# Strips written out in place of a loop, and gates spread by pairs of experts into a ring of six pairs

## The chip, the cores and the metric

The kernel runs on one core of one Trainium2 chip. A core has five engines that run side by side, each with its own list of instructions: TensorE (PE in the profile; its weight loads are PEld), VectorE (DVE), ScalarE (ACT), GpSimd (POOL) and SyncE (SP), which here issues every DMA. They wait for each other by semaphores. The metric is the device time of the whole program in microseconds (us), the median of several runs.

## The reference

The input x has the shape (4, 64, 128, 128). Two residual blocks are applied to it, window attention and a mixture of experts:

```python
x = x + attention(_ln_c(x), ...)      # 8x8 windows, 4 heads of 16 channels, relative position bias
t = _to_tokens(x)                     # 4 x 16384 tokens of 64 channels
t = t + ffn(_ln_t(t), ...)

# ffn
router_probs = softmax(x @ router_w + router_b)      # 8 experts
top_p, top_i = top_k(router_probs, 2)
top_p = top_p / sum(top_p)
expert_out = einsum('bnd,edc->bnec', x, expert_w) + expert_b
out = einsum('bnk,bnkc->bnc', top_p, take_along_axis(expert_out, top_i[..., None], axis=2))
```

All arithmetic is in float32. `_ln_c` and `_ln_t` take the mean away over the channels and divide by the standard deviation.

## The kernel before

**Strips.** The work is cut into 32 strips. A strip is eight rows (one row of windows) of two images; the two images' channels take the 128 partitions (image `a` has partitions 64a to 64a+63), and the 8 x 128 = 1024 pixels lie along the row (`LT`). A strip passes through seven stages, and in each step of the program every engine works on up to seven strips, `s[0]` to `s[6]`, where `s[k]` is the strip that was loaded k steps ago. `s[2]` and `s[3]` are in attention, `s[4]` gets its residual, its router and its gates, `s[5]` goes through the experts and is finished, `s[6]` is stored. There are 38 steps. Each engine's order within a step is written out by hand in its last function (L376, L625, L814, L918, L1108).

**The loop.** `steps` (L264) writes out steps 0 to 9, runs steps 10 to 29 as a hardware loop of five rounds of U = 4 steps, and writes out steps 30 to 37. In the loop the values that semaphores are waited for depend on the round, so registers are computed, and x is loaded and stored at addresses from registers. There are four jumps back.

**Gates.** For each token the two chosen experts have a gate and the other six have zero. The chain that makes them, per strip: TensorE transposes the router's output (`transpose_logits`, L588), VectorE finds the top two (L1060 to L1106), GpSimd places the gates (`place_gates`, L898 to L909), TensorE transposes them (`transpose_gates`, L595 and L597), ScalarE moves them to SBUF (`move_gates`, L812), SyncE writes them to DRAM (`write_gates`, L329) and reads them back, each expert's row of 1024 gates copied to all 64 partitions of its image (`spread_gates`, L347). The tile `gz` has eight buffers of one expert each. Per expert there are two DMAs, one for each image, of 64 rows of 4 KB. Then the token tile `tt` is multiplied into the buffer in place (`gated`): experts 1, 4 and 7 on GpSimd (L915), 0, 2, 3, 5 and 6 on VectorE (L1026). TensorE multiplies each expert's buffer by its weights and adds all up in PSUM (`experts`, L620), and `finish` (L1034) adds the residual.

**Order around it.** On VectorE the end of a step is `normalise` 3, `gated` 0, `finish` of the strip before, `gated` 2; the next step begins with `row_max` 2 (L1005), `shift` 2 (L1012), `gated` 3, `gated` 5, `variance` (L986). On TensorE a step begins with `experts` 0, transposes and channel sums, `scores_left` 3 (L516, which needs `shift` 2), values, the router, `scores_right` 3, transposes, `transpose_logits` (L588, which needs a PSUM bank that `variance` frees). GpSimd does the residual (L889), `gated` 1, `gated` 4, later `place_gates` and `gated` 7. On SyncE the spreads of experts 0 to 5 end the step, and 6 and 7 begin the next one, followed by the store, the load of x, `swap_tokens` and `load_gate_rows`.

## Time and profile before

| | us |
|---|---|
| median of 3 runs | 1319.18 |
| lowest and highest | 1318.9, 1325.99 |
| the profiled execution | 1319.76 |
| its span, first to last instruction | 1317.8 |
| TensorE, VectorE busy | 1108.7 (84%), 920.3 (70%) |
| ScalarE, GpSimd busy | 707.6 (54%), 439.8 (33%) |
| SyncE's DMA queue | 217.32 MB, 66.3% of 16 DMA engines |
| mean granted TensorE clock | 0.934 |

No engine is busy all the time; the strips' chains through several engines and the DMA queue set the pace. A step is best read from one mark per step, for instance the start of ScalarE's move of the projection (L779), and within a step from T, the start of the first DMA that spreads the strip's gates. The granted clock is 1.0 at 2.4 GHz and 0.5 at 1.2 GHz.

### The profile page before, as it was taken

How to read it: one execution, taken by the hardware profiler on the slowest of the kernel's cores; microseconds unless marked ns; L12 is line 12 of the kernel's file. 1: busy time of each engine (PE TensorE's matmuls, PEld its weight loads, DVE VectorE, ACT ScalarE, POOL GpSimd, SP SyncE). 2: the span in 40 equal slices, each digit the busy share in tenths (PEclk: the TensorE clock that was granted, in tenths of full speed). 3: DMA queues.
4: the chain of work that ended last, by engine and by line, in shares of the span. 5: the costliest groups of instructions: out<-in, count | busy, mean ns of one | idle time of the engine just before them, and what ended most of it. 6: DMA issues, size and time to landing. Idle time of an engine off the chain costs nothing.

```text
span 1317.8 us, 41226 instructions
## 1 busy us (share of the span) xinstructions
PE 1108.7 (84%) x16678; PEld 578.2 (44%) x16678; DVE 920.3 (70%) x1398; ACT 707.6 (54%) x1153; POOL 439.8 (33%) x359
## 2 busy tenths in 40 slices
PE   4688998888899979987998879899799889988754
PEld 2344444444444434443544435444344444444311
DVE  3247787778777767885778757777677877776642
ACT  1366565555565646654665546665466566555410
POOL 1003234433443233343234424432343344233342
PEclk9999899999999989998999989999899999998877
DMA  3216676777766658877576777776588777755676
GB/s 127 65 42 155 147 183 174 179 199 189 197 159 173 174 143 199 198 195 188 123 184 171 180 183 190 169 177 173 136 199 200 194 188 162 172 146 143 153 174 169
DMA packets 91494, 219.85 MB, mean 167 GB/s; under 512 B 17728, under 2 KB 30656, under 8 KB 91200
## 3 DMA queue, kind: packets, MB, share of 16 engines
q1 hardware_dynamic: 91328, 217.32, 66.3%
q8 instruction: 143, 2.34, 0.8%
q14 instruction: 23, 0.19, 0.1%
HBM read 177.15 MB, written 23.33 MB: 152 GB/s over the span
## 4 chain that ended last, share of the span: by engine, by line
PE 44%; DMA 26%; issue 11%; SPq 9%; DVE 6%; ACT 2%; POOL 1%; POOLq 0%; DVEq 0%; ACTq 0%
DMA gz<-gates_dram 22%; PE bank L620 14%; SPq L347 8%; PE bank L501 6%; PE bank L462 5%; PE bank L534 5%; PE bank L551 3%; PE bank L558 3%; DMA gates_dram<-gsb 3%; PE bank L489 3%; PE bank L516 2%; DVE mx L1005 2%; DVE probs L1012 2%; PE bank L588 2%; DVE gz L1026 1%
## 5 line engine op out<-in xcount | busy, mean ns | idle before, releaser
L1026 DVE TENSOR_TENSOR gz<-gz,tt 128x1024 f32<-128x1024 f32 x160 | 301.6, 1889 | 127.3 <-DMA gz<-gates_dram 127.2
L620 PE MATMUL bank<-gz,wex 64*64 64x512 f32 x2048 | 276.8, 648 | 47.7 <-issue 33.2
L915 POOL TENSOR_TENSOR gz<-gz,tt 128x1024 f32<-128x1024 f32 x96 | 250.4, 2619 | 23.9 <-DMA gz<-gates_dram 23.9
L889 POOL TENSOR_TENSOR tt<-prj,xs 128x512 f32<-128x512 f32 x64 | 106.3, 1681 | 437.1 <-ACT prj L779 437.1
L762 ACT ACTIVATE pt<-bank 128x512 f32<-128x512 f32 x256 | 150.5, 588 | 106.4 <-PE bank L534 106.4
L1005 DVE TENSOR_REDUCE mx<-bank 128x16 f32<-128x1024 f32 x128 | 155.6, 1216 | 58.4 <-PE bank L501 58.4
L1012 DVE TENSOR_TENSOR probs<-bank,mx 128x1024 f32<-128x1024 f32 x128 | 156.7, 1224 | 43.3 <-PE bank L534 34.3
L501 PE MATMUL bank<-km,qs 32*64 32x128 f32 x4096 | 177.7, 289 | 3.4 <-issue 0.5
L534 PE MATMUL bank<-cst,probs 128*128 128x128 f32 x1024 | 173.3, 293 | 5.1 <-ACT pt L762 5.1
L501 PEld LDWEIGHTS bank<-km,qs 32*64 32x64 f32 x4096 | 113.4, 136 | 111.4 <-issue 100.1
L534 PEld LDWEIGHTS bank<-cst,probs 128*128 128x128 f32 x1024 | 110.7, 144 | 114.3 <-issue 48.0
L898 POOL TENSOR_TENSOR ga<-oh,g 128x128 f32<-128x128 f32 x32 | 13.9, 434 | 400.9 <-DVE g L1106 400.9
L620 PEld LDWEIGHTS bank<-gz,wex 64*64 64x64 f32 x2048 | 71.8, 142 | 171.3 <-issue 169.7
L516 PE MATMUL bank<-bias_hl,tile_id 128*128 128x512 f32 x256 | 93.3, 447 | 60.0 <-DVE probs L1012 54.6
L755 ACT ACTIVATE probs<-probs 128x1024 f32<-128x1024 f32 x128 | 134.8, 1053 | 6.9 <-DVE probs L1012 6.2
L769 ACT ACTIVATE rden<-bank 128x256 f32<-128x256 f32 x128 | 49.1, 383 | 109.4 <-PE bank L558 109.4
L551 PE MATMUL bank<-pt,vbd 128*32 128x64 f32 x4096 | 94.5, 229 | 1.5 <-ACT pt L762 1.5
L1020 DVE TENSOR_TENSOR onrm<-bank,rden 128x256 f32<-128x256 f32 x128 | 54.0, 422 | 52.0 <-ACT rden L774 51.7
L462 PE MATMUL bank<-xr,wcen 64*64 64x512 f32 x512 | 74.2, 655 | 10.1 <-DVE var L986 5.8
L558 PE MATMUL bank<-pt,cst 128*32 128x256 f32 x1024 | 80.2, 385 | 0.0
L740 ACT ACTIVATE km<-bank,hmask 128x1024 f32<-128x1024 f32 x64 | 67.8, 1110 | 23.0 <-PE bank L462 23.0
L551 PEld LDWEIGHTS bank<-pt,vbd 128*32 128x32 f32 x4096 | 67.2, 113 | 28.4 <-issue 23.5
(95 smaller groups left out, 1259.8 us busy)
## 6 DMA issues: line engine op xcount, KB each, us to landing
gz<-gates_dram SPq DMA_DIRECT2D x512, 256.0 KB, 7.9
xs<-in_x SPq DMA_DIRECT2D x32, 512.0 KB, 10.6
rstd<-std_dram SPq DMA_DIRECT2D x64, 256.0 KB, 4.0
tx<-tt SPq DMA_DIRECT2D x128, 128.0 KB, 9.2
out<-ob SPq DMA_DIRECT2D x128, 128.0 KB, 9.1
gates_dram<-gsb SPq DMA_DIRECT2D x32, 192.0 KB, 2.1
grow<-gates_dram SPq DMA_DIRECT2D x192, 32.0 KB
gz<-in_rel SPq DMA_DIRECT2D x1, 2048.0 KB, 8.8
```

The lines of the kernel that those rows point to most:

```text
L462: last = mm(bank[64 * x:64 * x + 64, PRE + a, :], wcen[64 * a:64 * a + 64, at + 64 * a:at + 64 * a + 64], xr[s.buf(2)][64 * a:64 * a + 64, ...
L501: last = mm(bank[N * j:N * j + N, S_BANK + hp, 256 * x + 128 * ii:256 * x + 128 * ii + 128], qs[32 * r:32 * r + 32, a, w, :], km[32 * r:32 ...
L534: last = nc.tensor.transpose(bank[:, PT_BANK, 128 * r:128 * r + 128], probs[g % 2][:, r % 2, r // 2, u % 2, :], cv("ident"))
L551: mm(bank[32 * r:32 * r + 32, OD_BANK, at:at + N], vbd[:, CW * (r // 2) + w, 2 * a + r % 2, :, :].rearrange("p m d -> p (m d)"), pt[g % 2] ...
L558: last = mm(bank[32 * r:32 * r + 32, OD_BANK, 256:512], cv("pair"), pt[g % 2][:, :, r, :, :], start=True, stop=True, skip_group_check=True)
L620: last = mm(bank[64 * x:64 * x + 64, Y_BANK + a, :], wex[64 * a:64 * a + 64, e, :], gz[64 * a:64 * a + 64, e, x * CH:(x + 1) * CH], start= ...
L755: af(v, v, ACT.Exp).then_inc(exp_done, 1)
L762: af(pt[g % 2][:, u % 2, :, :, :].rearrange("p r j q -> p (r j q)"), bank[:, PT_BANK, :], ACT.Copy).then_inc(pt_ready, 1)
L915: tt_(gz[:, e, :], gz[:, e, :], tt[s.buf(4)][:, :], op=ALU.mult).then_inc(z_pool, 1)
L1005: red(mx[g % 2][:, :], two_banks(S_BANK).rearrange("p (c k) -> p c k", k=N), axis=AX_X, op=ALU.max).then_inc(max_done, 1)
L1012: tt_(probs[g % 2][:, :, :, :, :].rearrange("p h x i (m k) -> p (h x i m) k", k=N), two_banks(S_BANK).rearrange("p (c k) -> p c k", k=N), ...
L1026: tt_(gz[:, e, :], gz[:, e, :], tt[s.buf(4)][:, :], op=ALU.mult).then_inc(z_dve, 1)
```

## The change

Three things are changed, and the order of work on each engine stays.

1. All 38 steps are written out. The loop, its registers, its jumps and the semaphores `waited` and `sp_waited` are gone, and all waits are for constants.
2. `gz` has six buffers of two experts each (48 KB of a partition in place of 32 KB). Pair q of strip c uses buffer (4c + q) mod 6. Per pair there are two DMAs, one for each image, of 64 rows of 8 KB, so eight DMAs for a strip in place of sixteen. `gated` waits for the pair that holds its expert. A pair's load waits until the pair that had the buffer six pairs earlier has been used up.
3. To make room, `lnv`, `L2` and `cand` are dropped: `msq`, `Ls` and `eq` are written again in their place.

```diff
-        gz = sb("gz", [P, E, LT])
+        gz = sb("gz", [P, GZ_RING, 2, LT])
...
+            def pair(self, e):
+
+                return divmod(4 * self.c + e // 2, GZ_RING)
...
-            for i in range(lo):
-                run(Step(i, 0, False))
-            with nc.Fori(0, n, engines=(run.engine,)) as r:
-                for v in range(U):
-                    run(Step(lo + v, r, True))
-            for i in range(lo + n * U, last + 1):
-                run(Step(i, 0, False))
...
+        def stepped(f):
+            for c in range(STRIPS + LAST_STAGE):
+                f(Step(c))
+            return f
...
-            def spread_gates(s, e):
-
-                if e == 0:
+            def spread_gates(s, q):
+
+                if q == 0:
                     sp.wait_ge(gates_written, s.count(16, 16))
-                    sp.sem_inc(sp_waited, 1)
-                wait(sp, e_done, s.count(E, e + 1, lag=1))
+
+                wait(sp, e_done, 2 * (s.count(4, q) - GZ_RING + 1))
+                k = s.count(4, q) % GZ_RING
                 for a in range(2):
-                    sp.dma_start(gz[64 * a:64 * a + 64, e, :],
-                                 gates_dram[s.buf(4), 0, E * a + e, :].partition_broadcast(64)
-                                 ).then_inc(gz_loaded[e], 16)
+                    sp.dma_start(gz[64 * a:64 * a + 64, k, :, :].rearrange("p e t -> p (e t)"),
+                                 gates_dram[s.buf(4), 0, E * a + 2 * q:E * a + 2 * q + 2, :].rearrange(
+                                     "e t -> (e t)").partition_broadcast(64)).then_inc(gz_loaded[k], 16)
...
                 if s[5].on:
-                    spread_gates(s[5], 6)
-                    spread_gates(s[5], 7)
+                    spread_gates(s[5], 3)
...
-                pool.wait_ge(gz_loaded[e], s.count(32, 32))
-                tt_(gz[:, e, :], gz[:, e, :], tt[s.buf(4)][:, :],
+                use, k = s.pair(e)
+                pool.wait_ge(gz_loaded[k], 32 * use + 32)
+                tt_(gz[:, k, e % 2, :], gz[:, k, e % 2, :], tt[s.buf(4)][:, :],
                     op=ALU.mult).then_inc(z_pool, 1)
...
-                dve.wait_ge(gz_loaded[e], s.count(32, 32))
-                tt_(gz[:, e, :], gz[:, e, :], tt[s.buf(4)][:, :],
+                use, k = s.pair(e)
+                dve.wait_ge(gz_loaded[k], 32 * use + 32)
+                tt_(gz[:, k, e % 2, :], gz[:, k, e % 2, :], tt[s.buf(4)][:, :],
                     op=ALU.mult).then_inc(z_dve, 1)
```

**The queue of SyncE.** First one written-out step of before, from the write of the gates to DRAM, then the same place now:

```order
L329 DMA gates_dram<-gsb 128x3x128
L347 DMA gz<-gates_dram 64x1024 x16
L367 DMA out<-ob 64x512 x4
L308 DMA xs<-in_x 128x1024
L356 DMA tx<-tt 64x512 x4
```

```order
L304 DMA gates_dram<-gsb 128x3x128
L323 DMA gz<-gates_dram 64x2048 x8
L343 DMA out<-ob 64x512 x4
L284 DMA xs<-in_x 128x1024
L332 DMA tx<-tt 64x512 x4
```

Nothing has moved; sixteen DMAs of 64 x 1024 elements have become eight of 64 x 2048.

**VectorE around the step's boundary**, a written-out place, with the semaphores that each row waits for (`gz_loaded2` belongs to expert 2 before, and to the buffer that pair 2 of one strip or another uses now). Before:

```order
L1026 TENSOR_TENSOR gz<-gz,tt3 128x1024 [waits gz_loaded0]
L1034 TENSOR_TENSOR ob0<-bank,tx 128x1024 [waits stored0,tx_loaded0,y_full]
L1026 TENSOR_TENSOR gz<-gz,tt3 128x1024 [waits gz_loaded2]
L1005 TENSOR_REDUCE mx0<-bank 128x16 [waits s_full]
L1012 TENSOR_TENSOR probs0<-bank,mx0 128x1024 [waits t_full,max_done]
L1026 TENSOR_TENSOR gz<-gz,tt3 128x1024 [waits gz_loaded3]
L1026 TENSOR_TENSOR gz<-gz,tt3 128x1024 [waits gz_loaded5]
L986 TENSOR_TENSOR var<-bank,msq 128x256 [waits std_written,msq_ready]
```

Now (the strip shown uses the buffers 0, 1 and 2 for its pairs 0, 1 and 2):

```order
L997 TENSOR_TENSOR gz<-gz,tt3 128x1024 [waits gz_loaded0]
L1005 TENSOR_TENSOR ob0<-bank,tx 128x1024 [waits stored0,tx_loaded0,y_full]
L997 TENSOR_TENSOR gz<-gz,tt3 128x1024 [waits gz_loaded1]
L975 TENSOR_REDUCE mx0<-bank 128x16 [waits s_full]
L982 TENSOR_TENSOR probs0<-bank,mx0 128x1024 [waits t_full,max_done]
L997 TENSOR_TENSOR gz<-gz,tt3 128x1024 [waits gz_loaded1]
L997 TENSOR_TENSOR gz<-gz,tt3 128x1024 [waits gz_loaded2]
L956 TENSOR_TENSOR var<-bank,msq 128x256 [waits std_written,msq_ready]
```

The order is the same. The first `gated` now waits for experts 0 and 1 together, the second for 2 and 3, the fourth for 4 and 5.

**TensorE at the loop's end**, before:

```order
L534 MATMUL bank<-cst,probs 128x128 x4
L524 REGISTER_ALU
L501 MATMUL bank<-km,qs 64x128 x8
L271 REGISTER_ALU
L271 COMPARE_AND_BRANCH
L620 MATMUL bank<-gz,wex 64x512 x4
```

Now there is no register operation and no branch between the steps; the matmuls stand in the same order.

## Rows read from the trace of the kernel before

**Rows 1.** The page: shares of engines and of the chain that ended last.

```profile
PE 1108.7 (84%) x16678; PEld 578.2 (44%) x16678; DVE 920.3 (70%) x1398; ACT 707.6 (54%) x1153; POOL 439.8 (33%) x359
PE 44%; DMA 26%; issue 11%; SPq 9%; DVE 6%; ACT 2%; POOL 1%; POOLq 0%; DVEq 0%; ACTq 0%
DMA gz<-gates_dram 22%; PE bank L620 14%; SPq L347 8%; PE bank L501 6%; PE bank L462 5%; PE bank L534 5%; PE bank L551 3%; PE bank L558 3%; DMA gates_dram<-gsb 3%; PE bank L489 3%; PE bank L516 2%; DVE mx L1005 2%; DVE probs L1012 2%; PE bank L588 2%; DVE gz L1026 1%
```

**Rows 2.** Timeline of ScalarE, L779, once per step: start, duration, what, [idle before].

```profile
196.94 1.11 ACT L779 ACTIVATE prj<-bank,sml 128x1024 f32<-128x1024 f32 x1 [0.75 <-PE bank L569]
...
346.88 1.11 ACT L779 ACTIVATE prj<-bank,sml 128x1024 f32<-128x1024 f32 x1 [0.75 <-PE bank L569]
...
612.28 1.11 ACT L779 ACTIVATE prj<-bank,sml 128x1024 f32<-128x1024 f32 x1 [0.75 <-PE bank L569]
...
654.62 1.11 ACT L779 ACTIVATE prj<-bank,sml 128x1024 f32<-128x1024 f32 x1 [0.76 <-PE bank L569]
...
1073.08 1.11 ACT L779 ACTIVATE prj<-bank,sml 128x1024 f32<-128x1024 f32 x1 [0.75 <-PE bank L569]
...
1223.00 1.11 ACT L779 ACTIVATE prj<-bank,sml 128x1024 f32<-128x1024 f32 x1 [0.75 <-PE bank L569]
```

**Rows 3.** A jump back: TensorE's timeline, and its line in the waits.

```profile
621.74 1.98 PE L620 MATMUL bank<-gz,wex 64*64 64x512 f32 x8 [8.34 <-issue]
...
PE bank L620 <- issue: 33.2, 5, 8.3
```

**Rows 4.** Timeline of SyncE's queue in one step, from T = 338.47, and its wait there.

```profile
335.96 0.41 SPq L329 DMA_DIRECT2D gates_dram<-gsb  x1
338.47 10.99 SPq L347 DMA_DIRECT2D gz<-gates_dram  x16
349.72 2.53 SPq L367 DMA_DIRECT2D out<-ob  x4
352.56 0.37 SPq L308 DMA_DIRECT2D xs<-in_x  x1
...
375.78 0.45 SPq L347 DMA_DIRECT2D gz<-gates_dram  x1
...
SPq L347 <- PE bank L620: 10.1, 22, 1.4
```

**Rows 5.** DMA in windows 340.3:340.7, then 342.9:343.3: issue to landing of one DMA.

```profile
gz<-gates_dram SPq DMA_DIRECT2D x1, 256.0 KB, 5.5
...
gz<-gates_dram SPq DMA_DIRECT2D x1, 256.0 KB, 8.6
```

**Rows 6.** VectorE's timeline in the same step.

```profile
343.51 1.23 DVE L1026 TENSOR_TENSOR gz<-gz,tt 128x1024 f32<-128x1024 f32 x1
344.86 1.23 DVE L1034 TENSOR_TENSOR ob<-bank,tx 128x1024 f32<-128x1024 f32 x1
349.17 1.34 DVE L1026 TENSOR_TENSOR gz<-gz,tt 128x1024 f32<-128x1024 f32 x1 [3.08 <-DMA gz<-gates_dram]
350.43 1.21 DVE L1005 TENSOR_REDUCE mx<-bank 128x16 f32<-128x1024 f32 x1
351.76 1.22 DVE L1012 TENSOR_TENSOR probs<-bank,mx 128x1024 f32<-128x1024 f32 x1
352.90 2.13 DVE L1026 TENSOR_TENSOR gz<-gz,tt 128x1024 f32<-128x1024 f32 x1
355.80 2.55 DVE L1026 TENSOR_TENSOR gz<-gz,tt 128x1024 f32<-128x1024 f32 x1 [0.76 <-DMA gz<-gates_dram]
358.27 0.41 DVE L986 TENSOR_TENSOR var<-bank,msq 128x256 f32<-128x256 f32 x1
```

**Rows 7.** GpSimd's timeline in the same step: experts 1 and 4.

```profile
351.60 2.35 POOL L915 TENSOR_TENSOR gz<-gz,tt 128x1024 f32<-128x1024 f32 x1
...
353.91 3.35 POOL L915 TENSOR_TENSOR gz<-gz,tt 128x1024 f32<-128x1024 f32 x1
```

**Rows 8.** TensorE's timeline there, and ScalarE's row of the gates.

```profile
353.04 0.73 PE L516 MATMUL bank<-bias_hl,tile_id 128*128 128x512 f32 x2 [1.85 <-DVE probs L1012]
...
356.12 0.66 PE L534 MATMUL bank<-cst,probs 128*128 128x128 f32 x4
358.83 1.08 PE L588 MATMUL bank<-cst,lg 128*128 128x128 f32 x4 [2.06 <-DVE var L986]
...
373.04 0.49 ACT L812 ACTIVATE gsb<-bank 128x384 f32<-128x384 f32 x1
```

**Rows 9.** A shorter step: half clock ahead of L588 (last row: windows, clock 0.50).

```profile
508.43 0.92 PE L516 MATMUL bank<-bias_hl,tile_id 128*128 128x512 f32 x2 [1.85 <-DVE probs L1012]
...
513.05 0.66 PE L534 MATMUL bank<-cst,probs 128*128 128x128 f32 x4
514.21 0.63 PE L588 MATMUL bank<-cst,lg 128*128 128x128 f32 x4 [0.51 <-DVE var L986]
...
526.98 0.49 ACT L812 ACTIVATE gsb<-bank 128x384 f32<-128x384 f32 x1
...
508.80:512.21 3.41, 3.41 (x42) 1.36 (x40) 2.97 (x2) 0.07 (x1) 3.41 (x2) 0.50 1.04 231
```

**Rows 10.** DMA packets in windows 303:318, 320:322 and 9:13.

```profile
DMA packets 1076, 3.55 MB, mean 237 GB/s; under 512 B 213, under 2 KB 213, under 8 KB 1075
...
DMA packets 340, 0.81 MB, mean 405 GB/s; under 512 B 57, under 2 KB 57, under 8 KB 339
...
DMA packets 122, 1.72 MB, mean 430 GB/s; under 512 B 8, under 2 KB 8, under 8 KB 20
```

More of the change, by code:

```diff
@@ L47, in build_program @@
     PAIRS = B // 2
+    GZ_RING = 6
     LAST_STAGE = 6
@@ L210, in build_program @@
         gates_written, grow_loaded = sem("gates_written"), sem("grow_loaded")
-        gz_loaded = [sem(f"gz_loaded{e}") for e in range(E)]
+        gz_loaded = [sem(f"gz_loaded{k}") for k in range(GZ_RING)]
         z_dve, z_pool, e_done, y_full, y_ready = (sem("z_dve"), sem("z_pool"), sem("e_done"), sem("y_full"),
@@ L227, in build_program, with __init__ @@
         }
-        class Step:
-            def __init__(self, c, n, inner):
-                self.c, self.n, self.inner = c, n, inner
-            def strips(self):
-                return [Strip(self.c - k, self.n, self.inner) for k in range(LAST_STAGE + 1)]
         class Strip:
-            def __init__(self, c, n, inner):
-                self.c, self.n, self.inner = c, n, inner
-                self.on = inner or 0 <= c < STRIPS
+            def __init__(self, c):
+                self.c = c
+                self.on = 0 <= c < STRIPS
             def buf(self, k):
@@ L248, in count, with __init__, strips @@
             def count(self, per, k, lag=0):
-                v = per * (self.c - lag) + k
-                return v + per * U * self.n if self.inner else v
+                return per * (self.c - lag) + k
             def rounds(self, k, of):
-                v = of * (self.c // k)
-                return v + of * (U // k) * self.n if self.inner else v
-        def wait(eng, s, value):
-            if isinstance(value, int) and value <= 0:
-                return
-            eng.wait_ge(s, value)
-        def steps(run):
-            last = STRIPS - 1 + LAST_STAGE
-            lo = LAST_STAGE + 4
-            n = (STRIPS - lo) // U
-            for i in range(lo):
-                run(Step(i, 0, False))
-            with nc.Fori(0, n, engines=(run.engine,)) as r:
-                for v in range(U):
-                    run(Step(lo + v, r, True))
-            for i in range(lo + n * U, last + 1):
-                run(Step(i, 0, False))
-        def stepped(engine_type):
-            def mark(f):
-                class Run:
-                    engine = engine_type
-                    def __call__(self, st):
-                        f(st)
-                steps(Run())
-            return mark
+                return of * (self.c // k)
+            def pair(self, e):
+                return divmod(4 * self.c + e // 2, GZ_RING)
+        class Step:
+            def __init__(self, c):
+                self.c = c
+            def strips(self):
+                return [Strip(self.c - k) for k in range(LAST_STAGE + 1)]
+        def wait(eng, s, value):
+            if value > 0:
+                eng.wait_ge(s, value)
+        def stepped(f):
+            for c in range(STRIPS + LAST_STAGE):
+                f(Step(c))
+            return f
         block = ctx.enter_context(nc.Block())
-        ET = mybir.EngineType
         @block.sync
@@ L374, in late_loads @@
                     sp.dma_start(dst, src).then_inc(late_loaded, 16)
-            @stepped(ET.SP)
+            @stepped
             def _(st):
@@ L439, in free @@
                     _, back, s, per = rounds[at]
-                    if st.inner or 0 <= c - back < STRIPS:
-                        wait(pe, s, Strip(c - back, st.n, st.inner).count(per, per))
+                    if 0 <= c - back < STRIPS:
+                        wait(pe, s, Strip(c - back).count(per, per))
                         return
@@ L1089, in top_two @@
             def top_two(s):
-                top_step(s, 10, nc.vector.scalar_tensor_tensor(out=L2[:, :, :], in0=oh1[:, :, :], scalar=-BIG,
+                top_step(s, 10, nc.vector.scalar_tensor_tensor(out=Ls[:, :, :], in0=oh1[:, :, :], scalar=-BIG,
                                                                in1=L[:, :, :], op0=ALU.mult, op1=ALU.add))
-                candidates(s, 10, L2, m2)
+                candidates(s, 10, Ls, m2)
             def pick_two(s):
```

41 lines of the change are left out of this document (14 added, 27 removed).

## The prediction

> **What bounds the kernel now.** I read the page first. TensorE is busy 84% and VectorE 70%, so neither fills the span, and the chain that ended last holds 22% of DMA of the spread gates and 8% of their issue beside TensorE's lines [rows 1]. So each strip's gates go round a circle, and the circle's length is a step. The next view is one mark per step. Eight written-out steps on either side of the loop (196.94 to 346.88 and 1073.08 to 1223.00) take 299.86 us, 37.48 each. The 19 steps between, which hold the loop's jumps, take 726.20 us, where 19 at 37.48 would be 712.1. One step with a jump takes 654.62 - 612.28 = 42.3 us [rows 2], and TensorE idles 8.34 us in it without a releaser; 33.2 us of such idle time stand in the waits, five times, four of them jumps [rows 3].
>
> Then the circle itself, in one step, with T = 338.47, the first spread DMA [rows 4]. Expert 1 lands at 340.24 + 5.5 = T+7.3, expert 3 at 342.80 + 8.6 = T+12.9 (issued in the 10.99 us burst, one DMA each 0.64 us) [rows 4, 5]. VectorE multiplies expert 0 at T+5.0, finishes the older strip by T+7.6, waits 3.08 us for expert 2 until T+10.7, does the maximum and the shift until T+14.5, expert 3, waits 0.76 us for expert 5 until T+17.3, and starts the variance at T+19.8 [rows 6]. TensorE waits twice: 1.85 us for the shift, starting at T+14.6, and 2.06 us for the variance, until L588 at T+20.4. From L588 the top two, the gates and their transposes lead to L812 at 373.04, which is 14.2 us later [rows 8], and 2.74 us after that the next strip's spread starts, at 375.78 [rows 4]. 20.4 + 14.2 + 2.7 = 37.3. Both of VectorE's waits end with a landing, so landings set the circle.
>
> **The clock in it.** In a step in the loop L588 comes only 0.51 us after its predecessor, because TensorE ran at clock 0.50, 1.2 GHz, from 508.80 to 512.21, after its 1.85 us wait; from there to L812 it is 526.98 - 514.21 = 12.8 us, not 14.2 [rows 9]. So a stretch at half clock costs some 1.4 us behind L588 and nothing ahead of it, where the wait for the variance hides it. The written-out steps have mostly the first kind.
>
> **Part 1, the loop written out.** The matmuls and their order are the same, and the written-out steps of before already show what steps without a jump cost. Replacing the 19 looped steps by steps of 37.48 us removes 726.2 - 712.1 = 14.1 us. That is less than four times 42.3 - 37.5 = 4.8, since some looped steps after a jump are short ones of 36.1, with the half clock hidden. Registers and added semaphore steps cost nothing that I can see: the looped steps without a jump are no longer than written-out ones. The trace shows the stall at the jump itself as 8.34 us of idle TensorE [rows 3]. The Trainium skill, in "Runtime: NRT & Kernel Launch", section "Instruction fetch mechanics", says that a taken branch breaks the sequential prefetch; the trace agrees with it, but adds that half of the stall is caught up.
>
> **Part 2, pairs: what falls away.** Eight DMAs fewer are issued per strip, at 0.64 us each 5.1 us of SyncE's queue. I cost this at nothing. The DMA engines are the cover: over 303 to 318 they move 237 GB/s [rows 10], so the strip's 4.19 MB take 17.7 us, longer than the issue's 11. Behind the burst on SyncE stands the store, which must wait for `finish` (which part 3 ends at T+10.6) and starts at T+11.2 today, so the queue gains no time for it; x and the tokens queue behind the same bytes. The wait for a free buffer is gone too: it was 10.1 us over the whole run, in 22 pieces [rows 4], and the same backlog hid it. The aliases of `msq`, `Ls` and `eq` join operations that already follow each other on one engine, and cost nothing.
>
> **Part 3, pairs: what comes later.** Bytes and order are kept, so pair q lands when its second expert landed: pair 0 at T+7.3 (7.3 to 8.4 over the strips), pair 1 at T+12.9, pair 2 at T+17.3, as expert 5 does. The steps on VectorE are then:
> - `gated` 0 starts at T+8.0 in place of 5.0, `finish` ends at T+10.6. `experts` 0 on TensorE, which follows the free PSUM bank, slips by 0.9 us into the wait for the shift, where it is hidden; if that wait were gone it would cost its 0.9.
> - `gated` 2 starts at T+12.9 in place of 10.7. It now lies beside `gated` 1 on GpSimd, so I take 2.13 us for it, as `gated` 3 had beside GpSimd, not 1.34 [rows 6, 7]. Then maximum and shift, 2.4 us: T+17.4 in place of 14.5. TensorE's first wait grows from 1.85 to about 3.5 us.
> - `gated` 4 on GpSimd starts with pair 2, at T+17.3 in place of 15.4, and takes 3.35 us beside VectorE: T+20.7. `gated` 3 runs to T+19.5, and `gated` 5 ends 1.1 us after GpSimd's operation, as it does now (358.35 against 357.26): T+21.7 [rows 6, 7]. The variance starts there, and L588 0.56 us later: T+22.3 in place of 20.4.
> So the wait of 0.76 is gone, but the operations are squeezed behind a later pair 1 and a later `gated` 4: +1.9 us on this leg.
>
> **What the clock gives back.** TensorE's work between its two waits is 3.7 us at full clock (353.04 to 356.78) [rows 8] and 5.3 us with the half clock in it (508.43 to 513.71) [rows 9]. With one long wait ahead of it the half clock moves mostly ahead of L588. Then L588 is at the later of T+22.3 and 17.5 + 5.3 = T+22.8, and the circle is 22.8 + 12.8 + 2.7 = 38.3. With the stretch hidden partly in the long wait it is 22.3 + 12.8 + 2.7 = 37.8; with it behind L588 still, 39.2. I take 38.05, between the first two, since the wait becomes longer than either was. Over about 28 steps (the first and last few have fewer stages) this is 28 x (38.05 - 37.48) = +16 us.
>
> **Sum.** 1319.76 - 14.1 + 16 = 1321.7 for the profiled execution, which stands 0.6 above the median of the three; I say **1321**, no change. The unknown that counts most is the rate at which rows of 8 KB move. From above, 430 GB/s: one broadcast DMA of 16 KB rows to 128 partitions had it [rows 10]. From below, half of that, 215. I stay at 237, by the nearest row: the same 64-partition broadcasts. Each per cent of it moves pair 2 by 0.13 us and the run by 3.7 us.
>
> On that rate two rules can be weighed. The broadcast to all 128 partitions moved 430 GB/s, and the two broadcasts to 64 each only 237, at full DMA share in both [rows 10]. The Trainium skill, "DMA: Bandwidth & Descriptors", section "The descriptor swizzle", has the partitions 0 to 63 behind one half of the ports and 64 to 127 behind the other; by this a 64-partition DMA has half of the ports whatever its row's length, and the sum stays.
>
> **The rivals.**
> - *Rows of 8 KB move faster* (faster). For it: packets of 4 KB move at 237 GB/s, of 16 KB at 430 [rows 10], and eight completions per strip fall away. Against: those 16 KB went to 128 partitions, and 405 GB/s were reached at 320 to 322 by stores and x with rows of 2 and 4 KB. With 10% more, pair 1 lands at T+11.9 and pair 2 at T+16.0; L588 follows at 20.9 to 21.8, a circle of 36.5 to 37.3, and the run at 1319.8 - 14.1 - 28 x 0.6 = 1289. By the Trainium skill, "DMA: Bandwidth & Descriptors", section "Rules for kernel authors", bigger DMAs have more bandwidth; that would be this rival.
> - *The later landing is absorbed* (faster). If the half clock falls wholly into the long wait and VectorE and GpSimd hinder each other less, the circle stays at 37.5, and the loop's share is left: 1319.8 - 14.1 = 1306.
> - *The two halves' packets overlap less* (slower). 237 is over 215, so today the packets for the lower and the upper 64 partitions overlap somewhat. With four packets of 8 KB per DMA and engine they may do so for a smaller share. At 222 GB/s pair 2 lands 0.9 us later, all of it is on the leg, and the half clock can fall behind L588: a circle of 39.1 and 1319.8 - 14.1 + 28 x 1.6 = 1350. It decides from a rate under 233, where the steps add over 0.5%.
> - *The written-out code stalls*: each engine streams more code. The written-out steps show no idle time of this kind; a stall in each of 20 steps of 1 us would give 1341.
>
> **How the numbers follow.** Forecast 0.45, with a range of its own of 1310 to 1334; of it 0.30 within 0.5%, 0.12 slower, 0.03 faster. Faster rows 0.22; absorbed 0.10; less overlap 0.19, code 0.04. A measurement of this kernel can tell about 0.5% from no change, 6.6 us. Faster 0.35, same 0.30, slower 0.35. The range 1288 to 1348 takes in the likelier parts of both sides and leaves a tenth out at either end.
>
> **What would show it.** After the change no idle time of 8 us at a step's start. VectorE's idle time before `gated` 0 and `gated` 2 by landings at T+8 and T+12.9, none before `gated` 5; one wait of TensorE of over 3 us at L516 and under 1 us at L588; `gated` 4 at pair 2's landing; the rate in the burst at 237. A rate above 250 or below 230 makes the forecast wrong, and so would steps of another length at the same landings.

## The result, and the profile after

The changed kernel takes **1367.16 us** (median, 1365.24 to 1367.37) where the kernel before takes 1321.96 in the same comparison: a ratio of 1.034, with an interval of 1.030 to 1.037. It is slower, and outside the predicted range of 1288 to 1348. The profiled execution has a span of 1363.3 us, 45.5 more than before. Executions of one kernel fall into a faster and a slower state, and ratios go by the faster ones; the profiled executions of two runs below, e3 (1273.2 us) and e10 (1354.9 us), and one more of e3's four runs, were slower ones.

The page of the changed kernel, in the order of [rows 1]: busy time of engines, then the chain that ended last. After it, the kind of transfer that is spread per pair, with the KB and the median us from issue to landing.

```profile
PE 1121.5 (82%) x16678; PEld 591.5 (43%) x16678; DVE 947.2 (69%) x1398; ACT 709.3 (52%) x1153; POOL 408.6 (30%) x359
...
PE 43%; DMA 33%; DVE 8%; issue 7%; SPq 5%; ACT 2%; POOL 1%; POOLq 0%; DVEq 0%
...
gz<-gates_dram SPq DMA_DIRECT2D x256, 512.0 KB, 12.0
```

The DMA's share of the chain has risen from 26% to 33%. TensorE is busy 13 us more than before, VectorE 27 us more and GpSimd 31 us less, at the same work. The marks of the steps (ScalarE's move of the projection, as [rows 2]):

```profile
203.61 1.11 ACT L748 ACTIVATE prj<-bank,sml 128x1024 f32<-128x1024 f32 x1 [0.75 <-PE bank L539]
242.38 1.11 ACT L748 ACTIVATE prj<-bank,sml 128x1024 f32<-128x1024 f32 x1 [0.75 <-PE bank L539]
282.36 1.12 ACT L748 ACTIVATE prj<-bank,sml 128x1024 f32<-128x1024 f32 x1 [0.75 <-PE bank L539]
321.11 1.11 ACT L748 ACTIVATE prj<-bank,sml 128x1024 f32<-128x1024 f32 x1 [0.75 <-PE bank L539]
...
1265.49 1.12 ACT L748 ACTIVATE prj<-bank,sml 128x1024 f32<-128x1024 f32 x1 [0.75 <-PE bank L539]
```

Most steps alternate between 38.8 us and 39.5 to 40.0. Over the same 27 steps, (1265.49 - 203.61)/27 = 39.33, where before had (1223.00 - 196.94)/27 = 38.00 [rows 2]. So 45.5 splits into 35.8 in the 27 steps (1.33 each), 6.7 ahead of the first mark and 3.0 behind the last.

Now one step, with T = 352.15, the start of the first spread DMA. SyncE's queue, as [rows 4]:

```profile
350.07 0.39 SPq L304 DMA_DIRECT2D gates_dram<-gsb  x1
352.15 4.92 SPq L323 DMA_DIRECT2D gz<-gates_dram  x8
361.87 2.85 SPq L343 DMA_DIRECT2D out<-ob  x4
```

VectorE, as [rows 6], and GpSimd, as [rows 7]:

```profile
359.48 1.23 DVE L997 TENSOR_TENSOR gz<-gz,tt 128x1024 f32<-128x1024 f32 x1 [1.83 <-DMA gz<-gates_dram]
360.62 1.22 DVE L1005 TENSOR_TENSOR ob<-bank,tx 128x1024 f32<-128x1024 f32 x1
365.28 2.80 DVE L997 TENSOR_TENSOR gz<-gz,tt 128x1024 f32<-128x1024 f32 x1 [3.44 <-DMA gz<-gates_dram]
368.01 1.21 DVE L975 TENSOR_REDUCE mx<-bank 128x16 f32<-128x1024 f32 x1
369.25 1.22 DVE L982 TENSOR_TENSOR probs<-bank,mx 128x1024 f32<-128x1024 f32 x1
370.39 4.37 DVE L997 TENSOR_TENSOR gz<-gz,tt 128x1024 f32<-128x1024 f32 x2
374.69 0.41 DVE L956 TENSOR_TENSOR var<-bank,msq 128x256 f32<-128x256 f32 x1
```

```profile
364.64 2.37 POOL L885 TENSOR_TENSOR gz<-gz,tt 128x1024 f32<-128x1024 f32 x1
370.19 2.36 POOL L885 TENSOR_TENSOR gz<-gz,tt 128x1024 f32<-128x1024 f32 x1 [3.19 <-DMA gz<-gates_dram]
```

`gated` 0 starts at T+7.3 and `finish` ends at T+9.7. `gated` 2 starts at T+13.1 and ends at 368.08, T+15.9; that is 1.07 us after the end of GpSimd's `gated` 1 (367.01), which ran beside it. The shift ends at T+18.3. TensorE then, as [rows 8], in this step and the next (whose T is 390.98). L487 is `scores_left` 3 and L558 is `transpose_logits`, which were L516 and L588 before. ScalarE's move of the gates to `gsb` and the windows of both stretches at half clock follow (the last three columns are clock, DMA share and GB/s):

```profile
370.53 1.22 PE L487 MATMUL bank<-bias_hl,tile_id 128*128 128x512 f32 x2 [5.24 <-DVE probs L982]
...
375.73 0.60 PE L558 MATMUL bank<-cst,lg 128*128 128x128 f32 x4
...
409.36 1.22 PE L487 MATMUL bank<-bias_hl,tile_id 128*128 128x512 f32 x2 [5.23 <-DVE probs L982]
...
415.50 0.60 PE L558 MATMUL bank<-cst,lg 128*128 128x128 f32 x4
```

```profile
388.38 0.49 ACT L781 ACTIVATE gsb<-bank 128x384 f32<-128x384 f32 x1
...
428.15 0.49 ACT L781 ACTIVATE gsb<-bank 128x384 f32<-128x384 f32 x1
```

```profile
367.36:374.20 6.84, 3.67 (x42) 1.86 (x42) 6.80 (x5) 0.00 (x0) 2.36 (x1) 0.50 0.98 235
...
408.30:415.14 6.84, 5.78 (x59) 2.81 (x60) 5.61 (x5) 1.14 (x2) 2.36 (x1) 0.50 1.00 288
```

TensorE waits 5.24 us for the shift in place of 1.85 [rows 8], and the wait for the variance is gone. It then runs at 1.2 GHz until 374.20 in the first step, and until 415.14 in the second. L558 therefore starts at T+23.6 in the one and T+24.5 in the other; 12.65 us lie from there to `gsb` in both, and 2.6 from `gsb` to the next T: 38.8 and, within 0.1, 39.8 us, the two lengths of the steps. So the circle that the prediction read is longer at two places, the end of `gated` 2 and the half clock.

The waits of the whole run (total us, times, longest), the second of them 54.6 in the kernel before; and the DMA packets of one burst, as [rows 10]:

```profile
DVE gz L997 <- DMA gz<-gates_dram: 198.6, 67, 13.4
...
PE bank L487 <- DVE probs L982: 135.9, 34, 5.2
POOL gz L885 <- DMA gz<-gates_dram: 124.7, 34, 8.6
```

```profile
DMA packets 494, 3.27 MB, mean 218 GB/s; under 512 B 96, under 2 KB 96, under 8 KB 96
```

218 GB/s where there were 237 [rows 10]. Over strips 3 to 28 the pairs land at T+7.7, 13.2, 18.1 and 22.4 on average; before, experts 1, 3, 5 and 7 landed at 7.9, 12.8, 17.3 and 20.9.

### The profile page after: what moved, and what is told of

It reads as the page before. It is cut to its first block, busy times and chain, and to the rows that moved or that the text cites. A ratio compares the mean times of both kernels' runs of the same rounds, so it can differ in the third digit from the quotient of the medians.

```text
span 1363.3 us, 38803 instructions
## 1 busy us (share of the span) xinstructions
PE 1121.5 (82%) x16678; PEld 591.5 (43%) x16678; DVE 947.2 (69%) x1398; ACT 709.3 (52%) x1153; POOL 408.6 (30%) x359
## 4 chain that ended last, share of the span: by engine, by line
PE 43%; DMA 33%; DVE 8%; issue 7%; SPq 5%; ACT 2%; POOL 1%; POOLq 0%; DVEq 0%
DMA gz<-gates_dram 27%; PE bank L589 10%; PE bank L472 7%; PE bank L505 6%; DMA gates_dram<-gsb 5%; SPq L323 4%; PE bank L433 4%; PE bank L487 4%; PE bank L522 4%; PE bank L548 3%; DVE probs L982 3%; DVE mx L975 3%; PE bank L529 2%; ACT gsb L781 1%; PE bank L558 1%
## 5 line engine op out<-in xcount | busy, mean ns | idle before, releaser
L997 DVE TENSOR_TENSOR gz<-gz,tt 128x1024 f32<-128x1024 f32 x160 | 325.1, 2047 | 198.8 <-DMA gz<-gates_dram 198.6
L589 PE MATMUL bank<-gz,wex 64*64 64x512 f32 x2048 | 262.8, 615 | 39.8 <-DVE ob L1005 33.4
L885 POOL TENSOR_TENSOR gz<-gz,tt 128x1024 f32<-128x1024 f32 x96 | 243.4, 2535 | 124.7 <-DMA gz<-gates_dram 124.7
L487 PE MATMUL bank<-bias_hl,tile_id 128*128 128x512 f32 x256 | 102.2, 484 | 143.0 <-DVE probs L982 135.9
L858 POOL TENSOR_TENSOR tt<-prj,xs 128x512 f32<-128x512 f32 x64 | 82.1, 1305 | 434.4 <-ACT prj L748 434.4
L472 PE MATMUL bank<-km,qs 32*64 32x128 f32 x4096 | 192.3, 308 | 2.9
L472 PEld LDWEIGHTS bank<-km,qs 32*64 32x64 f32 x4096 | 123.2, 146 | 129.1 <-issue 117.8
L759 ACT ACTIVATE lg<-bank 128x512 f32<-128x512 f32 x32 | 19.1, 597 | 238.2 <-PE bank L550 238.2
L589 PEld LDWEIGHTS bank<-gz,wex 64*64 64x64 f32 x2048 | 70.9, 135 | 159.7 <-issue 144.1
L487 PEld LDWEIGHTS bank<-bias_hl,tile_id 128*128 128x128 f32 x256 | 45.2, 210 | 163.5 <-DVE probs L982 154.1
L522 PE MATMUL bank<-pt,vbd 128*32 128x64 f32 x4096 | 97.5, 234 | 1.5 <-ACT pt L731 1.5
## 6 DMA issues: line engine op xcount, KB each, us to landing
xs<-in_x SPq DMA_DIRECT2D x32, 512.0 KB, 12.8
```

Of the source, the lines that this page charges most:

```text
L472: last = mm(bank[N * j:N * j + N, S_BANK + hp, 256 * x + 128 * ii:256 * x + 128 * ii + 128], qs[32 * r:32 * r + 32, a, w, :], km[32 * r:32 ...
L487: mm(bank[:, S_BANK + hp, :], tile_id[:, :], bias_hl[:, 2 * hp:2 * hp + 2, :].rearrange("p h k -> p (h k)").unsqueeze(1).broadcast_to([P, ...
L522: mm(bank[32 * r:32 * r + 32, OD_BANK, at:at + N], vbd[:, CW * (r // 2) + w, 2 * a + r % 2, :, :].rearrange("p m d -> p (m d)"), pt[g % 2] ...
L589: last = mm(bank[64 * x:64 * x + 64, Y_BANK + a, :], wex[64 * a:64 * a + 64, e, :], gz[64 * a:64 * a + 64, s.pair(e)[1], e % 2, x * CH:(x ...
L885: tt_(gz[:, k, e % 2, :], gz[:, k, e % 2, :], tt[s.buf(4)][:, :], op=ALU.mult).then_inc(z_pool, 1)
L997: tt_(gz[:, k, e % 2, :], gz[:, k, e % 2, :], tt[s.buf(4)][:, :], op=ALU.mult).then_inc(z_dve, 1)
```

## The experiments

Ratios are to the kernel before, run on the same chip; steps are means over the same 27 steps of the profiled execution.

| run | what it is | us | ratio, interval | steps |
|---|---|---|---|---|
| before | | 1319 | 1 | 38.0 |
| e11_ring8 | written out, eight single buffers | 1289.99 | 0.976, 0.971 to 0.981 | 37.2 |
| e1_single | the same, ring of twelve experts | 1296.13 | 0.980, 0.975 to 0.985 | 37.4 |
| e2_pairwait | e1, waits per pair | 1344.57 | 1.018, 1.012 to 1.023 | 38.9 |
| e10_quarter | after, 256 KB DMAs of 32 partitions | 1340.35 | 1.013, 1.009 to 1.018 | 39.0 |
| after | | 1367.16 | 1.034, 1.030 to 1.037 | 39.3 |

**e1_single: single experts, written out.** Does the loop or the spread make the difference?

```diff
-                for a in range(2):
-                    sp.dma_start(gz[64 * a:64 * a + 64, k, :, :].rearrange("p e t -> p (e t)"), ...)
+                for e in (2 * q, 2 * q + 1):
+                    wait(sp, e_done, 8 * s.c + e - 2 * GZ_RING + 1)
+                    for a in range(2):
+                        sp.dma_start(gz[64 * a:64 * a + 64, k, e % 2, :],
+                                     gates_dram[s.buf(4), 0, E * a + e, :].partition_broadcast(64)
+                                     ).then_inc(gz_loaded[2 * k + e % 2], 16)
```

> The written-out program with the ring kept (twelve single buffers), but each expert's gates are again two DMAs of 64 rows of 4 KB with a semaphore of their own. Both theories (the pairs' coarser waits cost the time; the pairs' lower DMA rate costs it) expect the same: steps of 37.5 us, a rate of 237 GB/s in the burst and 1306 us, within 1298 to 1320: the loop's share alone, 0.99 of before. A third theory, that the written-out code itself costs time, expects over 1340.

Measured: 1296.13 us, 0.980, just under what was expected (1298 to 1320), since the loop's share is larger. Landings and rate are those of before (expert 5 at T+17.1, 236 GB/s in the burst). So all of the loss is in the pairs, and they cost 71 us, not 16.

**e2_pairwait: DMAs per expert, waits per pair.** Of the pairs only the coarser wait is left.

```diff
-                                     ).then_inc(gz_loaded[2 * k + e % 2], 16)
+                                     ).then_inc(gz_loaded[k], 16)
...
-                dve.wait_ge(gz_loaded[2 * k + e % 2], 32 * use + 32)
+                dve.wait_ge(gz_loaded[k], 64 * use + 64)
```

> DMAs of 64 rows of 4 KB, one per expert and image as before, but the engines wait for both experts of a pair. Rate theory: the rate is 237 GB/s again, the pairs land at about T+7.6, 12.9 and 17.3, and only the grouping is paid, a circle of 38.2 to 38.6 us and 1325 to 1337 us in all. Grouping theory (the waits are the whole cost): 1355 to 1370 us, as the changed kernel.

Measured: 1344.57 us, 1.018, between what the two theories gave. The rate is that of before, and pairs land at T+8.1, 12.5 and 16.9 in the strip of T = 342.54. VectorE, GpSimd and TensorE in it:

```profile
355.05 3.44 DVE L998 TENSOR_TENSOR gz<-gz,tt 128x1024 f32<-128x1024 f32 x1 [2.04 <-DMA gz<-gates_dram]
358.41 1.21 DVE L976 TENSOR_REDUCE mx<-bank 128x16 f32<-128x1024 f32 x1
```

```profile
355.04 2.37 POOL L886 TENSOR_TENSOR gz<-gz,tt 128x1024 f32<-128x1024 f32 x1
```

```profile
360.93 1.06 PE L488 MATMUL bank<-bias_hl,tile_id 128*128 128x512 f32 x2 [4.52 <-DVE probs L983]
...
366.04 0.60 PE L559 MATMUL bank<-cst,lg 128*128 128x128 f32 x4
```

`gated` 2 starts at T+12.5 together with GpSimd's `gated` 1 and lasts 3.44 us, until T+15.9, as late as in the changed kernel although pair 1 lands 0.6 us sooner. The coarser wait alone costs 48 us.

`gated` 2 doesn't end so late in every step. GpSimd can start `gated` 1 at T+12.5, when the residual is done. In the strip of T = 693.94 pair 1 lands at T+12.42, just ahead of that, and VectorE gets in first (VectorE, GpSimd, TensorE):

```profile
706.39 1.23 DVE L998 TENSOR_TENSOR gz<-gz,tt 128x1024 f32<-128x1024 f32 x1 [2.03 <-DMA gz<-gates_dram]
```

```profile
706.44 3.38 POOL L886 TENSOR_TENSOR gz<-gz,tt 128x1024 f32<-128x1024 f32 x1
```

```profile
710.06 0.73 PE L488 MATMUL bank<-bias_hl,tile_id 128*128 128x512 f32 x2 [2.29 <-DVE probs L983]
```

Now VectorE's product takes 1.23 us and GpSimd's 3.38, and TensorE goes on at T+16.1 in place of 18.4. Of strips 3 to 28 this happens in five here, with steps of 36.3 to 37.7 us, in four of e10 below, and in none of the changed kernel, where pair 1 lands at T+12.7 or later.

**e4_rows4k: the changed kernel's eight DMAs with rows of 4 KB.** The buffer is laid out so that a pair's two experts aren't adjacent; DMAs, bytes and waits stay.

```diff
-        gz = sb("gz", [P, GZ_RING, 2, LT])
+        gz = sb("gz", [P, 2, GZ_RING, LT])
...
-                    sp.dma_start(gz[64 * a:64 * a + 64, k, :, :].rearrange("p e t -> p (e t)"), ...)
+                    sp.dma_start(gz[64 * a:64 * a + 64, :, k, :],
+                                 gates_dram[s.buf(4), 0, E * a + 2 * q:E * a + 2 * q + 2, :].partition_broadcast(64)
+                                 ).then_inc(gz_loaded[k], 16)
```

> The pairs' eight DMAs of 512 KB and the pairs' waits are kept, but a pair's two experts lie apart in SBUF, so each row is two packets of 4 KB. If the packet's length sets the rate: 237 GB/s again and 1325 to 1337 us. If the bytes that one DMA writes to one half of the partitions set it: 218 GB/s and 1360 to 1370 us, as the changed kernel.

Measured: 1363.57 us, 1.034 (1.031 to 1.037); pairs land at T+8.0, 13.5, 18.4 and 22.7. The packets' length is not the cause; the DMA of 512 KB is what e2 and e4 still differ in.

**e10_quarter: pieces of 256 KB with rows of 8 KB.** The other half of the same question.

```diff
-                for a in range(2):
-                    sp.dma_start(gz[64 * a:64 * a + 64, k, :, :].rearrange("p e t -> p (e t)"), ...)
+                for h in range(2):
+                    for a in range(2):
+                        sp.dma_start(gz[64 * a + 32 * h:64 * a + 32 * h + 32, k, :, :].rearrange("p e t -> p (e t)"),
+                                     ...partition_broadcast(32)).then_inc(gz_loaded[k], 16)
```

> The changed kernel, with each pair loaded by four DMAs of 32 partitions (256 KB each, rows of 8 KB as in the changed kernel), the two images in turn, in place of two DMAs of 64 partitions (512 KB). Theory: the size of the piece that goes to one half of the partitions before the other half's turn sets the rate. Then pieces of 256 KB bring back what e2_pairwait had: landings at T+7.9, 12.5, 17.0, 20.8, 237 GB/s in the burst, about 1345 us. Rival: rows of two experts or the coarser semaphore are slower whatever the piece is, or the 32 partitions are reached by fewer ports: landings as in the changed kernel or later (pair 2 at T+18 or more), 1362 us or more.

Measured: 1340.35 us, 1.013. The landings are e2's, T+7.6, 12.5, 17.0 and 20.9 (e2 has 7.9, 12.5, 17.0 and 20.8), and the burst has 237 GB/s again:

```profile
DMA packets 648, 3.56 MB, mean 237 GB/s; under 512 B 215, under 2 KB 215, under 8 KB 215
```

Rate and landings go with the size of the DMA, and so of the piece that each half of the partitions gets in turn, not with the rows; size and turns weren't varied apart. It costs 23 to 27 us (after against e2 and e10), each difference uncertain by some 8 us; between the profiled executions of e2 and the changed kernel it is 18. In e2's five steps in which VectorE got in first, 11 us are saved against 39.3, which is all that its 27 steps are shorter by (10.6). So read from these steps, the later landing costs time by losing this race, and not by its 0.7 us: where GpSimd is first at T+12.5, `gated` 2 ends at T+15.9, early landing or late.

**e11_ring8: the steps written out, without the larger ring.** As e1, with `GZ_RING = 4`, which is eight buffers. The reuse of `msq`, `Ls` and `eq` (part 3 of the change) stays.

> The steps written out and nothing else: eight buffers of one expert, DMAs and semaphores for each expert as in the kernel before (e1_single had twelve buffers). Theory: what e1_single gained (ratio 0.980, -23 us by its medians) is the loop's share alone, since the waits for a free buffer were 10 us in 22 pieces behind a backlog: 1293 to 1300 us, waits of SyncE for TensorE again at the spread. Rival: part of it is the ring's, and the loop's share is the 14 us of the prediction: 1305 to 1310 us.

Measured: 1289.99 us, 0.976, a little under the 1293 expected. The four more buffers of e1 bring nothing, and the loop's share is 22 us between the profiled executions (spans of 1317.8 and 1295.4) and 30 between the medians.

**e3_onesource: one DMA to all 128 partitions.** Both images get the first image's gates; the second image's own are left out.

```diff
-                for a in range(2):
-                    sp.dma_start(gz[64 * a:64 * a + 64, k, :, :].rearrange("p e t -> p (e t)"), ...)
+                sp.dma_start(gz[:, k, :, :].rearrange("p e t -> p (e t)"), ...
+                                 "e t -> (e t)").partition_broadcast(128)).then_inc(gz_loaded[k], 16)
```

> Each pair is one DMA with rows of 8 KB to all 128 partitions, from image 0's gates; the second image gets the first one's gates, which is left wrong, the bytes written are the same. Theory that a DMA to 64 partitions is held back by its destination half: the rate rises to 350 to 430 GB/s, pair 1 lands by T+8, pair 2 by T+11, VectorE waits for no landing after the first, and the time falls under 1290 us (steps of 35 to 36.5 us). Theory that many engines reading one source row hold it back: the rate stays near 220 GB/s and the time at 1355 to 1370 us.

Measured: 0.956 (0.948 to 0.964); the median of all four runs is 1271.35 us. Same bytes written, same rows of 8 KB, and the burst moves

```profile
DMA packets 735, 4.27 MB, mean 388 GB/s; under 512 B 95, under 2 KB 95, under 8 KB 255
```

with the last pair at T+14.8 in place of 22.4. So the 218 GB/s are a matter of the 64 partitions of one DMA, as far as this run tells: it also has half as many DMAs, of twice the size, and half as many source rows. By the Trainium skill, "DMA: Bandwidth & Descriptors", section "The descriptor swizzle", each half of the partitions has its own half of the ports, and this run agrees.

**e5_skew4k: the burst begun unevenly.** e1 with one DMA from DRAM to DRAM of 8 rows of 16 KB ahead of each burst.

```diff
+                    wait(sp, padded, s.count(16, 0))
+                    sp.dma_start(pad_dram, x_rows[0:8, 0:4096]).then_inc(padded, 16)
```

> The single-expert version (1296 us), with one DMA more ahead of each strip's burst, from DRAM to DRAM, of 8 rows of 16 KB (data that nobody uses), so that half of the DMA engines start the burst late by what one 64-partition DMA gives each engine. If the engines that share a destination port hinder each other because they are in step, the burst then moves at 350 to 430 GB/s, pair-wise landings come by T+6, T+8 and T+11, and the time falls by 5 to 30 us. If the engines fall back into step or do not pair like this, the rate stays at 237 GB/s and the time rises by the added issue, 0.5 us per step, 1296 to 1312.

Measured: 1301.34 us, 0.979 (0.969 to 0.988), expert 5 at T+17.2, 234 GB/s: nothing moves. The trace doesn't tell which DMA engine moved a packet, so whether the burst did begin unevenly isn't shown. This run rules out only that such a DMA ahead of it helps; how far two halves can overlap stays open.

**e6_swap: the changed kernel with `gated` 2 behind the shift.** VectorE's `gated` 2 moves from the end of a step behind the next step's `shift` 2.

```diff
                     shift(s[3], 2)
                 if s[5].on:
+                    gated(s[5], 2)
                     gated(s[5], 3)
                     gated(s[5], 5)
...
-                if s[4].on:
-                    gated(s[4], 2)
```

> The changed kernel with one move: VectorE's gated 2 goes behind the next step's row_max 2 and shift 2. Theory that the coarser wait costs because it stands ahead of the shift, on which TensorE waits 5.2 us: that wait falls to under 2 us at L487's place and the time to 1300 to 1330 us. Theory that the late pair 2 and gated 4 set the step: the variance stays at T+22 to 23, TensorE's wait moves to L558 and the time stays over 1350 us.

Measured: 1285.51 us, 0.974 (0.969 to 0.979), 82 below the changed kernel with the same transfers (pairs at T+7.6, 13.1, 17.9, 22.3). TensorE's wait for the shift is down from 135.9 us to 3.4; the wait for the variance is back:

```profile
PE bank L558 <- DVE var L956: 69.7, 28, 3.4
```

So the late pair 1 costs time because maximum and shift are queued behind it on VectorE. The 82 us are not the price of the pairs, since this move was not tried on single experts, where it could gain as well.

**e8_warm: TensorE kept busy in its wait.** The channel sums' first matmuls are issued seven times, so that the wait for the shift is partly filled.

```diff
-                for c in range(4):
-                    mm(bank[32 * c:32 * c + 32, PRE, 0:QT], cv("stat"), ...)
+                for _again in range(7):
+                    for c in range(4):
+                        mm(bank[32 * c:32 * c + 32, PRE, 0:QT], cv("stat"), ...)
```

> The changed kernel with the first four of the channel sums' matmuls made seven times in place of once (same result), 2.8 us more of TensorE's work just ahead of its 5.2 us wait for the shift. If the half clock that follows this wait is a part of the cost, the stretches of 6.8 us at 0.5 go or halve and the time falls by 20 to 45 us, to 1320 to 1347. If it is hidden anyway, the time stays at 1360 to 1372, or rises.

Measured: 1359.75 us, 1.029 (1.025 to 1.033). TensorE's idle time ahead of L488 falls to

```profile
PE bank L488 <- DVE probs L983: 66.8, 29, 4.9
```

and the mean granted clock rises from 0.921 to 0.936, which is half clock for 2 x 0.064 x 1362.6 = 174 us in place of 215. The median falls by 7 us, which is not clear of noise (the intervals overlap), and the span of the profiled execution by 0.7. Its steps fall from 39.33 to 39.04, which is 8 us over 27 of them, but the first mark comes 6 us later. So neither expectation is met cleanly: the half clock is not gone, the added matmuls take time themselves, and its price isn't settled by this.

**e7_order: off the circle altogether.** e1 with `gated` 2 behind `shift` 2, and `gated` 3 and 5 behind `guard_variance`, so that neither the shift nor the variance waits for a landing behind that of expert 0.

```diff
                 if s[5].on:
-                    gated(s[5], 3)
-                    gated(s[5], 5)
+                    gated(s[5], 2)
                 if s[1].on:
                     variance(s[1])
...
                     guard_variance(s[1])
+                if s[5].on:
+                    gated(s[5], 3)
+                    gated(s[5], 5)
...
-                if s[4].on:
-                    gated(s[4], 2)
```

> The single-expert version (1296 us) with VectorE's gated 2 behind shift 2, and gated 3 and 5 behind guard_variance, so that no landing stands ahead of the chain that makes the next strip's gates. If the circle through the landings sets the step, it is cut: steps of 34.5 to 36.5 us and 1230 to 1275 us. If another limit lies just under it (TensorE's half clock, VectorE's own work), 1280 to 1296 us.

Measured: 1188.55 us, 0.901 (0.897 to 0.905), faster than both kernels. Steps are 33.6 us, expert 5 still lands at T+17.1, and the clock is 0.985:

```profile
PE 1053.1 (89%) x16678; PEld 557.7 (47%) x16678; DVE 939.1 (79%) x1398; ACT 706.1 (60%) x1153; POOL 401.0 (34%) x359
...
PEclk9999999999999999999999999999999999999977
```

**e9_pairorder: the pairs in that order.**

> The changed kernel, pairs of experts in 512 KB DMAs and a semaphore for each pair, with VectorE's order of e7_order (expert 2 behind the second shift, experts 3 and 5 behind the guard of the variance). Theory: the pairs cost time only because VectorE waits for their later landings ahead of the shift and of the variance. Off that path they should cost next to nothing: steps of 33.4 to 34.0 us as in e7_order (33.6), landings of the pairs at T+7.7, 13.2, 18.1 and 22.4 as in the changed kernel, and 1190 to 1205 us. Rival: the DMA queue is the next bound, and with pairs it moves less per second; a strip moves 219.8 MB / 32 = 6.87 MB, which takes 31.4 us at the 219 GB/s of the pairs and leaves little room in 33.6: then steps of 35 us or more and 1230 us or more.

Its edit is e7's, made to the changed kernel. Measured: 1273.21 us, 0.965 (0.961 to 0.970), 85 above e7. The theory fails: steps vary from 34 to 40 us, with a mean of 36.3. The time is as the rival said (1230 or more); its reason isn't shown, since the DMA queue is no fuller than e7's (72.1% of the 16 engines' span, 72.7% in e7). In the step of T = 401.59, VectorE and TensorE:

```profile
409.05 1.22 DVE L997 TENSOR_TENSOR gz<-gz,tt 128x1024 f32<-128x1024 f32 x1 [3.89 <-DMA gz<-gates_dram]
410.19 1.22 DVE L1005 TENSOR_TENSOR ob<-bank,tx 128x1024 f32<-128x1024 f32 x1
```

```profile
411.55 1.09 PE L589 MATMUL bank<-gz,wex 64*64 64x512 f32 x8 [1.95 <-DVE ob L1005]
```

`gated` 0 waits for pair 0, `finish` is queued behind it, and TensorE's `experts` (L589, which was L620) waits for the bank that `finish` frees. In this step another landing has become the bound.

**e12_finishfirst and e13_quarterorder** each take one piece out of e9: the first puts `finish` ahead of `gated` 0, the second loads pairs in four DMAs as e10.

```diff
+                if s[5].on:
+                    finish(s[5])
                 if s[4].on:
                     gated(s[4], 0)
-                if s[5].on:
-                    finish(s[5])
```

> e9_pairorder with `finish` of the strip before ahead of `gated` 0 on VectorE. In e9 the pairs cost 85 us against the same order with single experts (1273 against 1189); its trace shows VectorE waiting 3.9 us for pair 0 in the step from T = 401.59, with `finish` queued behind, and TensorE idle 1.95 us for it. Theory: that queueing is most of the 85 us. Then `finish` starts at T+6.3 in place of 8.2 to 9.4, TensorE's wait for ob goes, steps fall from 36.3 to 34 or 35 us: 1205 to 1245 us. Rival: the cost is in the later pair 2 and in waits behind it (TensorE's wait for the products of experts 2 and 3, GpSimd's for expert 4 at T+18): then little changes, 1260 us or more.

> e9_pairorder with each pair loaded by four DMAs of 32 partitions and 256 KB, as in e10_quarter. Theory of the rate: the pieces of 512 KB hold the landings back by 0.7 us at pair 1, 1.1 at pair 2, 1.6 at pair 3; if that is most of what the pairs cost in this order, steps fall to 34 to 35 us and the time to 1205 to 1240 us. Rival: waiting for two experts instead of one is the cost, pair 0 still lands at T+7.6 and `gated` 0 waits for it: 1250 us or more.

Measured: 1249.61 us, 0.948 (0.942 to 0.953), and 1248.21, 0.947 (0.943 to 0.951). Each gives back 24 or 25 of the 85 us, and each lies between what its theory and its rival gave: both are a part, neither is most of it. The two together weren't tried; if their gains add up, the other 36 are open. In e12 TensorE still waits for VectorE's products,

```profile
PE bank L589 <- DVE gz L997: 73.3, 36, 7.3
```

where e7 has 36.2 us, and GpSimd waits 133.3 us for landings, where e7 has 49.5.

## Why the prediction was wrong

Between the profiled executions the split is measured: the loop -22.4 (1317.8 to 1295.4), the coarser wait +49.6 (to e2's 1345.0), the larger DMA +18.3 (to 1363.3). Each is one execution, and e2's four runs lie 15 us apart, so a few us can move between the terms. The forecast was -14.1, +16 and 0. The circle was the right one: with its landings off the path (e7) steps fall to 33.6 us. Of its terms these held and these failed.

- **The loop, part 1.** The idle times of 8 us at the jumps are gone, as said. The term was too small, 14.1 for 22 to 30. What failed here is the price of a written-out step, 37.48: e11 has 37.23 over 27 of them, since some are short (33.8 and 36.0 in its trace), and the eight written-out steps that the prediction averaged have none such.
- **Fewer DMAs and waits, part 2, gain nothing.** It holds as far as the runs tell: the issue of the spread ends 5 us after T, the store starts at T+9.7, and no step is shorter for it; e11 has the eight buffers' waits and isn't slower than e1.
- **Landings of pairs at 7.3, 12.9 and 17.3.** Right for pair 0 (7.7) and near for pair 1 (13.2); pair 2 is at 18.1. "I stay at 237, by the nearest row" was wrong: 218 to 221, by e4 and e10 because each DMA gives 512 KB to one half. The nearest row had the right partitions and rows of another length, but the size of the DMA is what counted.
- **`gated` 2 ends at T+15.0.** The step of the sum that failed most. Its 2.13 us came from `gated` 3 of [rows 6], which began 1.3 us into GpSimd's operation [rows 7]. Where both begin together VectorE's takes 3.44 (e2), since it ends about 1.05 us after GpSimd's. The prediction used just this for `gated` 5 and not for `gated` 2. `gated` 1 starts when the residual is done, at T+12.5 in most strips, so `gated` 2 ends at T+15.9 there in the changed kernel, e2, e4 and e10, though pair 1 lands between T+12.5 and 13.9. That is why TensorE mostly waits 4 to 5.2 us and not 3.5. Nor had the prediction asked which of the two starts first, and by e2 that is 2.3 us of a step.
- **The half clock hides ahead of L588.** From the wait's end to L558 the prediction had 5.3 us, and the trace has 5.2 in half of the steps. In the others the stretch at 1.2 GHz reaches to L558 and it is 6.1 (T+24.5). The rows of before had a stretch of 3.41 us in this place [rows 9], the changed kernel has 6.84 in both steps shown.
- **The circle.** 38.05 in the forecast, 39.33 measured. L588 was forecast at T+22.3 to 22.8 and is, as L558, at 23.6 and 24.5: 1.5 later in the middle, 0.9 of it by `gated` 2 and 0.6 by the clock; behind it stand 15.25 us, 0.25 less than forecast. The bound by `gated` 4 came 0.8 later, as pair 2 did (variance at T+22.5, 374.69, for T+21.7), and doesn't decide. Measured against e11's steps the pairs add 39.33 - 37.23 = 2.10 per step, not 0.57; the loop's larger share takes 0.25 of that back. 27 x 1.28 = 35 of the 44 us missed lie in the steps, the other 9 ahead of the first mark and behind the last, where the forecast took the pairs to cost next to nothing.
- **The rivals.** "The two halves' packets overlap less" came nearest: its rate of 222 and its pair 2 at +0.9 were met (218 to 221, +0.8), its circle of 39.1 nearly so. It held 0.19. But its reason, packets of 8 KB, fell with e4, and by e2 the rate is the smaller part, 18 of 68 us, so that its circle came out near is in part luck. "Rows of 8 KB move faster" fell. No stall of written-out code appeared. For the most bandwidth the Trainium skill, "DMA: Bandwidth & Descriptors", section "Rules for kernel authors", asks for 128 partitions and 1 MiB or more in one DMA. e3 had both, and its 388 GB/s agree; with 64 partitions the larger DMA alone went the other way, 218 GB/s with 512 KB and 237 with 256 KB.

## What to carry to other kernels

When a wait is made coarser, ask which operations of other strips stand behind it in the same engine's queue: here maximum and shift behind a product that no one needed yet, and moving that product (e6) was worth more than the whole change had cost. Price an operation that shares its time with another engine by which of the two starts first and where that one ends, not by a duration read in another place. Taking one landing off the path doesn't make a later landing free: the pairs cost 71 us in the first order and 85 in the better one.

## What the runs showed of the hardware

- A broadcast to 64 partitions in DMAs of 256 KB, the halves in turn, moved 234 to 237 GB/s with rows of 4 KB (e1, e5) and of 8 KB (e10); in DMAs of 512 KB it moved 218 to 221 with 8 KB (after) and 210 in one burst with 4 KB (e4), whose pairs land only 0.3 us after those of 8 KB. One DMA to all 128 partitions moved 388 (e3). By the Trainium skill, "SBUF — State Buffer", section "Can I just issue two DMAs to hit both halves?", two DMAs to different halves serialize, with 6% over a single one. No run here has a DMA to one half alone, but 218 to 237 GB/s in two halves is 0.56 to 0.61 of the 388 in one DMA, which agrees with halves that hardly overlap.
- A VectorE product that starts with a GpSimd product of the same size (2.37 us) takes 3.44 us and ends 1.08 after it; alone it takes 1.23 (359.48 in the changed kernel). Where VectorE's starts 0.05 us sooner (e2, 706.39), it takes 1.23, and GpSimd's 3.38. By the Trainium skill, "SBUF — State Buffer", section "SBUF: two separate sides", the two share a port pair by an exclusive lock, and the later one blocks for the whole instruction of the first; the trace agrees, since what is left behind the first one's end, 1.08 us and 2.20, is little less than the 1.23 and 2.37 of the product alone.
- Of the 33.2 us that TensorE idled in five pieces, four of them at jumps [rows 3], the steps written out gave back 22 to 30 us in all; the prediction had thought that half is caught up. That the rest came from these pieces alone isn't shown, since e11 also has steps of 33.8 us that the kernel before has not.
